# Shifted and seam copies of normalised image planes: by SBUF-to-SBUF DMAs instead of by VectorE

## The chip, the cores and the metric

One Trainium2 chip, one NeuronCore of it. The metric is the device time of one execution in microseconds, as the median of several executions. Engines by their names in the profile: PE (TensorE matmul) and PEld (its weight loads), DVE (VectorE), ACT (ScalarE), POOL (GpSimd) and SP (SyncE, which here only issues DMAs).

## The reference

The input x holds 32 images of 192 channels and 32 x 32 pixels. Each image goes through two residual blocks.

```python
x = x + _L0_conv_ref(_gn(x), w_qkv, w_out, b_out)        # channel attention
x = x + _L1_conv_ref(_gn(x), proj_w, proj_b, off_w, off_b, mask_w, mask_b, gamma, beta)
```

`_gn` is a group norm over 32 groups of channels. The first block forms a 192 x 192 attention matrix of channels per image. The second block is a deformable 3 x 3 convolution: an ordinary 3 x 3 convolution of the normalised image gives 27 numbers a pixel (two offsets and a mask for each of nine taps); each tap then reads the image at its shifted position with bilinear weights; the result is multiplied by `proj_w`, normalised over the whole batch (all images) and put through a GELU.

## The kernel before, in words

**Pipeline.** Images are handled in pairs of phases. `part0(u, b, par)` prepares image b: statistics, the attention block, the second group norm, the offset convolution and the bilinear weights. `part1(b, par, more)` does the deformable convolution of image b in 48 units (u = 0 to 47). In each unit, part1 of image b also calls `part0(u, b + 1, 1 - par)`, so the preparation of the next image is spread by hand over the units of this one. Image 0 is prepared alone, ahead of all. `par` is the parity of the image; buffers with a `par` index are doubled. Every engine runs its own copy of this order (lines 336 to 349), and semaphores tie the copies together. A hardware loop covers two images a turn.

**A unit of part1.** GpSimd multiplies row and column weights into `sT` (line 1323; one for two units, a ring of three). PE transposes it into `sps` (`turn_s`, line 650, done for unit u + 2), ACT rounds that to fp16 as `sh` (line 887), DVE subtracts to get the remainder `sl` (line 1142). PE then multiplies (lines 667 to 669). `sps` has two banks, so the transpose of unit u + 2 waits until `sl` of unit u is made (line 647). Beside this PE makes products of the planes with the projection weights, the z groups (lines 636 to 640), ten groups ahead; ACT and DVE split them likewise into `zh` (line 853) and `zl` (line 1136). From u = 38 on the z groups belong to the next image.

**The planes.** The second group norm of part0 gives the image as fp16 pieces in three planes of 128 partitions: `x2[0]` (first 128 channels, rounded), `x2[1]` (their remainder) and `x2[2]` (the other 64 channels, rounded in the lower half of the partitions, remainder in the upper). ACT writes the rounded pieces at units 30 to 33 and DVE the remainders, `residue`, at units 32 and 34 (line 999). Two more forms are needed. `x2s` has each plane moved by one pixel to the right and to the left within each image row, zero at the edge, for the left and right taps of the offset convolution. `x2w` has the last three and the first three rows of a plane side by side, for the z groups that lie across the image's seam. `move(k, b, par)` (line 1001) makes them with four DVE copies for plane k: lines 1005 and 1006 (31 of 32 columns of every row), 1008 and 1009 (seams). It is called at units 33, 35 and 36, ahead of nothing but the next unit's `sl` and `zl` in DVE's order:

```python
if u == 35:
    dve.wait_ge(xn_lo, 4 * b + 4)
    move(1, b, par)
if u == 36:
    move(2, b, par).then_inc(x2_moved, 1)
```

**Readers.** PE waits for `x2_moved` twice: before z group 0 of the next image, which reads `x2w` and which PE reaches in unit 38 of part1 (line 623), and before the offset convolution (line 572), 216 small matmuls (line 578) in units 38 and 39. From that follow, on the other engines, offsets, clipping, bilinear weights of the next image (lines 1096 to 1118 on DVE, 1307 on GpSimd).

**SP's queue** holds, for each image, in this order: `attended(b)`, the two stores of x1 and the three loads of the next image's x (at unit 26); and `convolved(b - 1)`, the two stores of y (line 431), which waits for unit 6 of the next part1.

**GpSimd** runs sT for the pairs of units p = 0 to 23, three ahead of PE at most; after the sT of pair p it does what `part0` has for units 2p - 4 and 2p - 3. At the start it zeroes the planes (line 1282).

Of the kernel before, what the change touches and what calls it, by code (L numbers as in the profile page):

```python
# [30 lines left out]
F32, F16, I32 = mybir.dt.float32, mybir.dt.float16, mybir.dt.int32  # L31
# [4 lines left out]
P = 128  # L36
C, H, W = 192, 32, 32
N = H * W
# [10 lines left out]
PAD_T, PAD_ROWS = 1, H + 2  # L49
WRAP = 3  # L50
# [32 lines left out]
def build(nc, x, w_qkT, w_v, w_outT, b_out, w_off, b_off, w_proj, proj_b, gamma, beta,  # L83
          avg, cy, cx, eye, out):
    NB = x.shape[0]
# [4 lines left out]
    with ExitStack() as ctx:  # L90
        def sb(name, shape, dt=F32):
            return ctx.enter_context(nc.sbuf_tensor(name, shape, dt))
# [4 lines left out]
        def sem(name):  # L97
            return ctx.enter_context(nc.semaphore(name))
# [48 lines left out]
        rsum = sb("rsum", [P, 2])  # L147
        rinv = sb("rinv", [P, 2])

        x2s = [sb(f"x2s_{n}", [P, 2, PAD_ROWS * W], F16) for n in ("hi_a", "lo_a", "hilo_b")]  # L150

        x2w = [sb(f"x2w_{n}", [P, 2, 2 * WRAP * W], F16) for n in ("hi_a", "lo_a", "hilo_b")]

        x2 = [sb(f"x2_{n}", [P, 2, PAD_ROWS * W], F16) for n in ("hi_a", "lo_a", "hilo_b")]
        off = sb("off", [P, 2, TILES, J])
        ay = sb("ay", [P, 2, TILES * TAPS, R])
        bx = sb("bx", [P, 2, TILES * TAPS, W])
# [66 lines left out]
        mx_ps = sem("mx_ps")  # L224
        x1_sb = sem("x1_sb")
        x1_stored = sem("x1_stored")
        x2_moved = sem("x2_moved")
        off_ps = sem("off_ps")
        off_sb = sem("off_sb")
# [58 lines left out]
        def inner(t, par):  # L288

            return t[:, par, PAD_T * W:PAD_T * W + N]  # L290
# [87 lines left out]
        def first(b):  # L378
            return isinstance(b, int) and b == 0
# [28 lines left out]
        @block.sync  # L408
        def _(sp):
            def load_x(b):  # L410
                for dst, src in ((xin[:, 0], x[b, 0:P]), (xin[0:CB, 1], x[b, P:C]), (xin[CB:P, 1], x[b, P:C])):
                    sp.dma_start(dst, src).then_inc(x_loaded, 16)

            load_blocks(sp, off_stage, w_off, weights_in)
            load_blocks(sp, proj_stage, w_proj, weights_in)
            sp.dma_start(eye32[:, :], eye).then_inc(const_in, 16)
            load_x(0)
            sp.dma_start(avg_sb[:, :, :], avg.rearrange("p (a b) -> p a b", a=4)).then_inc(const_in, 16)
            sp.dma_start(cy_sb[:, :], cy).then_inc(const_in, 16)
            sp.dma_start(cx_sb[:, :, :], cx.rearrange("p (k x) -> p k x", k=TAPS)).then_inc(const_in, 16)  # L420

            def attended(b, more=True):
                sp.wait_ge(x1_sb, 4 * b + 4)
                sp.dma_start(x1_dram[b, 0:P], x1[:, 0]).then_inc(x1_stored, 16)
                sp.dma_start(x1_dram[b, P:C], x1[0:CB, 1]).then_inc(x1_stored, 16)
                if more:
                    load_x(b + 1)

            def convolved(b):
                sp.wait_ge(y_final, b + 1)  # L430
                sp.dma_start(y_dram[b, 0:P], ych[:, 0]).then_inc(y_stored, 16)
                sp.dma_start(y_dram[b, P:C], ych[0:CB, 1]).then_inc(y_stored, 16)

            attended(0)
            with sp.Fori(1, NB - 2, 2) as b:
                attended(b)
                convolved(b - 1)
                attended(b + 1)
                convolved(b)
            attended(NB - 1, False)  # L440
            convolved(NB - 2)


            def load(dst, src, q, slot, i):
                if i < 2:
                    sp.dma_start(dst[slot][i], src[2 * q + i, 0:P]).then_inc(f_loaded[slot], 16)
                else:
                    for h in range(2):
                        sp.dma_start(dst[slot][i][CB * h:CB * h + CB], src[2 * q + h, P:C])\
                          .then_inc(f_loaded[slot], 16)  # L450

            def load_pair(q, slot):
                for i in range(3):
                    load(fin_y, y_dram, q, slot, i)
                    load(fin_x, x1_dram, q, slot, i)

            sp.wait_ge(y_stored, 32 * (NB - 2))
            sp.wait_ge(x1_stored, 32 * NB)
            sp.wait_ge(xn_hi, 4 * NB)
            for i in range(3):  # L460
                load(fin_y, y_dram, 0, 0, i)
            load(fin_x, x1_dram, 0, 0, 0)
            convolved(NB - 1)
            sp.wait_ge(bn_var, 1)
            for i in range(1, 3):
                load(fin_x, x1_dram, 0, 0, i)
            for slot in range(1, FIN):
                load_pair(slot, slot)
            sp.wait_ge(y_stored, 32 * NB)

            def load_next(r_, slot):
                sp.wait_ge(f_stored[slot], 64 * r_)
                load_pair(FIN * r_ + slot, slot)

            with sp.Fori(1, ROUNDS) as r_:
                for slot in range(FIN):
                    load_next(r_, slot)
            for slot in range(PAIRS - ROUND_ENDS):
                load_next(ROUNDS, slot)
# [455 lines left out]
        def _(dve):  # L935
# [62 lines left out]
                dve.wait_ge(xn_hi, 4 * b + 2 * n + i + 1)  # L998
                dve.tensor_tensor(lo, xn[:, 0] if i == 0 else xn[CB:P, 1], hi, ALU.subtract).then_inc(xn_lo, 1)

            def move(k, b, par):

                rows = lambda v: v.rearrange("p (h w) -> p h w", w=W)
                src = rows(inner(x2[k], par))
                dve.tensor_copy(rows(inner(x2s[k], 0))[:, :, 1:W], src[:, :, 0:W - 1])
                dve.tensor_copy(rows(inner(x2s[k], 1))[:, :, 0:W - 1], src[:, :, 1:W])
                seam = rows(x2w[k][:, par])
                dve.tensor_copy(seam[:, 0:WRAP], src[:, H - WRAP:H])
                return dve.tensor_copy(seam[:, WRAP:2 * WRAP], src[:, 0:WRAP])  # L1009

            def zero_outside(hat, rows, tiles):

                for t in tiles:
# [8 lines left out]
            def part0(u, b, par):  # L1022
# [54 lines left out]
                    group_variance(1, b)  # L1077
                if u == 32:
                    residue(0, inner(x2[1], par), inner(x2[0], par), 1, b)
                if u == 33:  # L1080
                    if not first(b):
                        dve.wait_ge(off_ps, b)
                    move(0, b, par)
                if u == 34:
                    residue(1, inner(x2[2], par)[CB:P], inner(x2[2], par)[CB:P], 1, b)
                if u == 35:
                    dve.wait_ge(xn_lo, 4 * b + 4)
                    move(1, b, par)
                if u == 36:
                    move(2, b, par).then_inc(x2_moved, 1)  # L1090
                if u == 40:
                    dve.wait_ge(off_ps, b + 1)
                    if not isinstance(b, int) or b >= 2:
# [184 lines left out]
        def _(pool):  # L1278
            pool.memset(mhalf[:, :], -0.5)
            pool.memset(minus[:, :], -1.0)  # L1280
            for t in (*x2, *x2s):
                ins = pool.memset(t[:, :, :], 0.0)
            ins.then_inc(pool_setup, 1)
            pool.wait_ge(pool_setup, 1)
            pool.wait_ge(const_in, CONST_DMAS * 16)
# [9 lines left out]
            def part0(u, b, par):  # L1295
                if u == 5:
                    group_rstd(0, b)
                if u == 29:
                    group_rstd(1, b)
                if u == 41:  # L1300
                    column_distance(0, b, par)

            def column_distance(q, b, par):
                if q == 0:
# [85 lines left out]
```

## Time and profile before

| What | Value |
|---|---|
| Median of 3 runs (lowest to highest) | 4268.0 us (4258.34 to 4275.98) |
| The profiled execution, first to last instruction | 4284.4 us |
| PE busy | 3630.2 us (85%) |
| DVE busy | 2649.3 us (62%) |
| ACT busy | 2110.5 us (49%) |
| POOL busy | 1410.9 us (33%) |
| Mean granted TensorE clock | 0.939 of full speed |
| DMA | 172.85 MB, mean 40 GB/s |

The profile shows one execution, 4284.4 us of span with no more than the launch around it, 16 us longer than the median run. Busy time is the share of the span in which an engine ran an instruction; PE's matmuls overlap, so its share says little of how near it is to its peak. A wait is idle time of an engine together with the instruction that released it; "issue" stands for time in which nothing that the profile shows held the engine.

### The profile page before, as it was taken

The numbers are of one execution on the slowest core, as the hardware profiler recorded it, in microseconds if no ns is written. First come the engines' busy times: TensorE is split into PE (matmuls) and PEld (weight loads), VectorE is DVE, ScalarE is ACT, GpSimd is POOL, SyncE is SP. The second block draws the span as 40 slices with busy tenths as digits, with TensorE's granted clock in tenths as the row PEclk, the third lists the DMA queues.
The fourth block names the chain that finished last, engine by engine and source line by source line (L and its number), as shares of the span: only waits on it lengthen the run. The fifth ranks groups of instructions, "written<-read, shape, count | busy, mean of one in ns | idle before, by whom it ended". The sixth has DMA issues, their size and how long they took to land.

```text
span 4284.4 us, 109949 instructions
## 1 busy us (share of the span) xinstructions
PE 3630.2 (85%) x38338; PEld 3094.4 (72%) x38338; DVE 2649.3 (62%) x5834; ACT 2110.5 (49%) x4790; POOL 1410.9 (33%) x1165
## 2 busy tenths in 40 slices
PE   3999898999989899998989989898998989899700
PEld 2787777877777778777777877777787777778700
DVE  3666666666666666666666666666666666666522
ACT  1555554555455455545545554554555455445432
POOL 1333332333333233333333333333333333333311
PEclk8999999999999999999999999999999999999955
DMA  2000000000000000000000000000000000000298
GB/s 59 18 27 10 28 27 20 27 27 27 10 27 27 20 27 26 27 10 27 27 20 27 26 27 16 21 27 20 27 26 27 21 16 27 27 20 16 60 361 301
DMA packets 50975, 172.85 MB, mean 40 GB/s; under 512 B 9664, under 2 KB 10880, under 8 KB 50176
## 3 DMA queue, kind: packets, MB, share of 16 engines
q1 hardware_dynamic: 39584, 136.75, 10.6%
q0 software_dynamic: 7168, 25.17, 1.5%
q8 instruction: 426, 6.98, 0.7%
q14 instruction: 373, 3.06, 0.2%
q10 hardware_dynamic: 3424, 0.90, 0.1%
HBM read 87.29 MB, written 75.50 MB: 38 GB/s over the span
## 4 chain that ended last, share of the span: by engine, by line
PE 63%; DVE 13%; issue 13%; ACT 4%; DMA 4%; DVEq 1%; ACTq 1%; SPq 1%; POOL 0%; POOLq 0%
PE sps L650 10%; PE acc L667 6%; PE acc L668 6%; PE acc L669 6%; PE l L578 4%; PE zps L636 3%; DVE zl L1136 3%; PE zps L640 3%; PE zps L637 3%; PE zps L638 3%; PE zps L639 3%; DMA xn<-x_scratch 2%; DVE sl L1142 2%; DVE ych L1204 2%; PE l L510 1%
## 5 line engine op out<-in xcount | busy, mean ns | idle before, releaser
L1323 POOL TENSOR_TENSOR sT<-ay,bx 128x768 f32<-128x768 f32 x768 | 1148.1, 1505 | 1615.3 <-PE sps L650 1547.9
L1142 DVE TENSOR_TENSOR sl<-sps,sh 128x384 f16<-128x384 f32 x1536 | 847.1, 552 | 743.7 <-ACT sh L887 740.3
L887 ACT CAST sh<-sps 128x384 f16<-128x384 f32 x1536 | 741.7, 483 | 915.4 <-PE sps L650 905.9
L667 PE MATMUL acc<-zh,sh 128*128 128x192 f16 x4608 | 1155.7, 251 | 0.3 <-ACT ypm L910 0.3
L668 PE MATMUL acc<-zl,sh 128*128 128x192 f16 x4608 | 1155.5, 251 | 0.0
L669 PE MATMUL acc<-zh,sl 128*128 128x192 f16 x4608 | 1155.2, 251 | 0.0
L650 PE MATMUL sps<-eye,sT 128*128 128x128 f32 x4608 | 808.0, 285 | 322.0 <-issue 218.2
L853 ACT CAST zh<-zps 128x288 f16<-128x288 f32 x1536 | 620.1, 404 | 699.6 <-PE zps L640 672.6
L1136 DVE TENSOR_TENSOR zl<-zps,zh 128x288 f16<-128x288 f32 x1536 | 693.9, 452 | 423.0 <-ACT zh L853 415.7
L650 PEld LDWEIGHTS sps<-eye,sT 128*128 128x128 f32 x4608 | 544.5, 143 | 451.9 <-issue 229.4
L667 PEld LDWEIGHTS acc<-zh,sh 128*128 128x128 f16 x4608 | 459.0, 100 | 37.5 <-issue 35.9
L668 PEld LDWEIGHTS acc<-zl,sh 128*128 128x128 f16 x4608 | 459.1, 100 | 20.9
L669 PEld LDWEIGHTS acc<-zh,sl 128*128 128x128 f16 x4608 | 459.1, 100 | 1.6
L636 PE MATMUL zps<-wpr_h,x_hi_a 128*128 128x288 f16 x1344 | 392.1, 292 | 0.8 <-DVE zl L1136 0.3
L637 PE MATMUL zps<-wpr_l,x_hi_a 128*128 128x288 f16 x1344 | 390.8, 291 | 0.0
L638 PE MATMUL zps<-wpr_h,x_lo_a 128*128 128x288 f16 x1344 | 390.1, 290 | 0.0
L639 PE MATMUL zps<-wpr_h,x_hilo_b 128*128 128x288 f16 x1344 | 389.7, 290 | 0.0
L640 PE MATMUL zps<-wpr_l,x_hilo_b 128*128 128x288 f16 x1344 | 389.7, 290 | 0.0
L1307 POOL TENSOR_TENSOR bx<-off,cx_sb 128x576 f32<-128x576 f32 x128 | 155.3, 1213 | 459.4 <-DVE off L1103 459.4
L1289 POOL TENSOR_TENSOR rstd<-gvar,mhalf 128x2 f32<-128x2 f32 x64 | 44.8, 700 | 582.0 <-DVE gvar L993 582.0
L578 PE MATMUL l<-wof,x2s_hi_a 128*128 128x54 f16 x1536 | 183.0, 186 | 9.8 <-DVE x2w_hilo_b L1009 9.8
L578 PE MATMUL l<-wof,x2s_lo_a 128*128 128x54 f16 x1536 | 182.8, 186 | 0.0
(200 smaller groups left out, 6498.0 us busy)
## 6 DMA issues: line engine op xcount, KB each, us to landing
xin<-in_x SPq DMA_DIRECT2D x32, 512.0 KB, 5.5
xin<-in_x SPq DMA_DIRECT2D x64, 256.0 KB, 5.9
x_scratch<-x SPq DMA_DIRECT2D x32, 512.0 KB, 2.8
y_scratch<-ych SPq DMA_DIRECT2D x32, 512.0 KB, 2.7
zh<-y_scratch SPq DMA_DIRECT2D x20, 512.0 KB, 11.0
zl<-x_scratch SPq DMA_DIRECT2D x20, 512.0 KB, 12.0
out<-zh POOLq DMA_DIRECT2D x20, 512.0 KB, 8.8
x_scratch<-x SPq DMA_DIRECT2D x32, 256.0 KB, 3.5
```

Of the source, the lines that this page charges most:

```text
L578: mm = pe.matmul(o, src[:, row * W:(row + ROWS_T) * W], wof[:, m, k].rearrange("p i j -> p (i j)"), start=(k == 0 and n == 0), stop=(k == ...
L636: pe.matmul(o, at(0), wpr_h[:, 0, ky, n], start=True, stop=False)
L637: pe.matmul(o, at(0), wpr_l[:, 0, ky, n], start=False, stop=False)
L650: mm = pe.transpose(sps[u % 2][:, kx * P:(kx + 1) * P], sT[:, g, kx, c * P:(c + 1) * P], eye32[:, :])
L667: pe.matmul(acc[:, 0:C], s_h, zh[:, j, ky, z], start=start and kx == 0, stop=False)
L668: pe.matmul(acc[:, 0:C], s_h, zl[:, j, ky, z], start=False, stop=False)
L669: mm = pe.matmul(acc[:, 0:C], s_l, zh[:, j, ky, z], start=False, stop=stop and kx == 2)
L853: act.copy(z_piece(zh, g, par), zps[:, g % 2, 0:KO // 2]).then_inc(z_hi, 1)
L887: act.copy(sh[:, u % S_RING].rearrange("p k n -> p (k n)"), sps[u % 2][:, 0:3 * P]).then_inc(s_hi, 1)
L1136: dve.tensor_tensor(z_piece(zl, g, par), zps[:, g % 2, 0:KO // 2], z_piece(zh, g, par), ALU.subtract)\
L1142: dve.tensor_tensor(one(sl), sps[u % 2][:, 0:3 * P], one(sh), ALU.subtract).then_inc(s_lo, 1)
L1323: pool.tensor_tensor(sT[:, p % ST_RING].rearrange("p k (r x) -> p k r x", r=R), a, x_, ALU.mult)\
```

## The change

The tensors of the three planes are joined into one tensor for each form, so that one access pattern takes all three planes. DVE's `move` is gone. SP, behind the x1 stores and the loads, waits for the last residue (`xn_lo`) and issues four DMAs: two for the seams, and two that copy the whole plane as one run of 1023 elements a partition and plane, one element to the right and one to the left. A run like that carries the last pixel of a row into the first column of the next one (or the reverse), so GpSimd, once all four have landed, sets that one column to zero in both moved forms with two memsets, and then raises `x2_moved`. PE's waits are as before.

```diff
-        x2s = [sb(f"x2s_{n}", [P, 2, PAD_ROWS * W], F16) for n in ("hi_a", "lo_a", "hilo_b")]
-
-        x2w = [sb(f"x2w_{n}", [P, 2, 2 * WRAP * W], F16) for n in ("hi_a", "lo_a", "hilo_b")]
-
-        x2 = [sb(f"x2_{n}", [P, 2, PAD_ROWS * W], F16) for n in ("hi_a", "lo_a", "hilo_b")]
+        x2s_all = sb("x2s", [P, 3, 2, PAD_ROWS * W], F16)
+        x2w_all = sb("x2w", [P, 3, 2, 2 * WRAP * W], F16)
+        x2_all = sb("x2", [P, 3, 2, PAD_ROWS * W], F16)
+        x2s, x2w, x2 = [[t[:, k] for k in range(3)] for t in (x2s_all, x2w_all, x2_all)]
...
+            def shift(b, par):
+
+                sp.wait_ge(xn_lo, 4 * b + 4)
+                plane = x2_all[:, :, par, PAD_T * W:PAD_T * W + N]
+                flat_plane = lambda h: x2s_all[:, :, h, PAD_T * W:PAD_T * W + N]
+                sp.dma_start(x2w_all[:, :, par, 0:WRAP * W], plane[:, :, N - WRAP * W:N]).then_inc(x2_shifted, 16)
+                sp.dma_start(x2w_all[:, :, par, WRAP * W:2 * WRAP * W], plane[:, :, 0:WRAP * W])\
+                  .then_inc(x2_shifted, 16)
+                sp.dma_start(flat_plane(0)[:, :, 1:N], plane[:, :, 0:N - 1]).then_inc(x2_shifted, 16)
+                sp.dma_start(flat_plane(1)[:, :, 0:N - 1], plane[:, :, 1:N]).then_inc(x2_shifted, 16)
+
...
             attended(0)
+            shift(0, 0)
             with sp.Fori(1, NB - 2, 2) as b:
                 attended(b)
+                shift(b, 1)
                 convolved(b - 1)
                 attended(b + 1)
+                shift(b + 1, 0)
                 convolved(b)
             attended(NB - 1, False)
+            shift(NB - 1, (NB - 1) % 2)
             convolved(NB - 2)
...
-            def move(k, b, par):
-
-                rows = lambda v: v.rearrange("p (h w) -> p h w", w=W)
-                src = rows(inner(x2[k], par))
-                dve.tensor_copy(rows(inner(x2s[k], 0))[:, :, 1:W], src[:, :, 0:W - 1])
-                dve.tensor_copy(rows(inner(x2s[k], 1))[:, :, 0:W - 1], src[:, :, 1:W])
-                seam = rows(x2w[k][:, par])
-                dve.tensor_copy(seam[:, 0:WRAP], src[:, H - WRAP:H])
-                return dve.tensor_copy(seam[:, WRAP:2 * WRAP], src[:, 0:WRAP])
...
-                if u == 33:
-                    if not first(b):
-                        dve.wait_ge(off_ps, b)
-                    move(0, b, par)
                 if u == 34:
                     residue(1, inner(x2[2], par)[CB:P], inner(x2[2], par)[CB:P], 1, b)
-                if u == 35:
-                    dve.wait_ge(xn_lo, 4 * b + 4)
-                    move(1, b, par)
-                if u == 36:
-                    move(2, b, par).then_inc(x2_moved, 1)
...
-            for t in (*x2, *x2s):
-                ins = pool.memset(t[:, :, :], 0.0)
+            for t in (x2_all, x2s_all):
+                ins = pool.memset(t[:, :, :, :].rearrange("p k h n -> p (k h n)"), 0.0)
...
+                if u == 37:
+                    edges(b)
                 if u == 41:
                     column_distance(0, b, par)
+
+            def edges(b):
+
+                pool.wait_ge(x2_shifted, 64 * b + 64)
+                pool.sem_inc(edges_due, 1)
+                for h in range(2):
+                    rows = x2s_all[:, :, h, PAD_T * W:PAD_T * W + N].rearrange("p k (r w) -> p k r w", w=W)
+                    ins = pool.memset(rows[:, :, :, (W - 1) * h:(W - 1) * h + 1], 0.0)
+                ins.then_inc(x2_moved, 1)
```

## Rows read from the trace of the kernel before

**Rows 1.** The page's head and its first part: busy time of each engine.

```profile
span 4284.4 us, 109949 instructions
PE 3630.2 (85%) x38338; PEld 3094.4 (72%) x38338; DVE 2649.3 (62%) x5834; ACT 2110.5 (49%) x4790; POOL 1410.9 (33%) x1165
```

**Rows 2.** Waits of PE: engine line waited for: us in total, times, longest.

```profile
PE sps L650 <- issue: 218.2, 46, 8.8
PE sps L650 <- DVE sl L1142: 96.1, 125, 1.2
```

**Rows 3.** DVE lines 999, 1005, 1008, 1009: duration ns min/median/max, first and last start.

```profile
L999 DVE TENSOR_TENSOR x_hilo_b<-xn,x_hilo_b x32: 1221/1222/1224, 94.0 to 3938.2; 64x1024 f16<-64x1024 f32 x32
...
L1005 DVE COPY x2s_hi_a<-x_hi_a x32: 408/410/419, 92.9 to 3935.2; 128x992 f16<-128x992 f16 x32
...
L1008 DVE COPY x2w_hi_a<-x_hi_a x32: 173/1446/1450, 93.6 to 3935.8; 128x96 f16<-128x96 f16 x32
...
L1008 DVE COPY x2w_hilo_b<-x_hilo_b x32: 163/167/173, 96.8 to 3944.0; 128x96 f16<-128x96 f16 x32
...
L1009 DVE COPY x2w_hilo_b<-x_hilo_b x32: 172/174/182, 96.9 to 3944.1; 128x96 f16<-128x96 f16 x32
```

**Rows 4.** Timeline of DVE, last image prepared: start us, us, instruction [idle before].

```profile
3935.16 0.41 DVE L1005 COPY x2s_hi_a<-x_hi_a 128x992 f16<-128x992 f16 x1
...
3937.30 0.54 DVE L1142 TENSOR_TENSOR sl<-sps,sh 128x384 f16<-128x384 f32 x1
```

**Rows 5.** Timeline of ACT in the same stretch.

```profile
3934.92 0.52 ACT L887 CAST sh<-sps 128x384 f16<-128x384 f32 x1
```

**Rows 6.** Timeline of PE in the same stretch; line 650 opens a unit.

```profile
3931.27 0.49 PE L650 MATMUL sps<-eye,sT 128*128 128x128 f32 x3
...
3932.95 0.49 PE L650 MATMUL sps<-eye,sT 128*128 128x128 f32 x3
...
3934.93 0.55 PE L650 MATMUL sps<-eye,sT 128*128 128x128 f32 x3
...
3937.90 0.55 PE L650 MATMUL sps<-eye,sT 128*128 128x128 f32 x3 [1.07 <-DVE sl L1142]
...
3943.08 0.55 PE L650 MATMUL sps<-eye,sT 128*128 128x128 f32 x3 [1.07 <-DVE sl L1142]
...
3944.40 0.29 PE L636 MATMUL zps<-wpr_h,x_hi_a 128*128 128x288 f16 x1
```

**Rows 7.** Timeline of SP: the two stores of y of one image.

```profile
3868.62 0.34 SPq L431 DMA_DIRECT2D y_scratch<-ych  x1
3869.17 0.54 SPq L432 DMA_DIRECT2D y_scratch<-ych  x1
```

**Rows 8.** DMA queues (packets, MB, share of 16 engines) and issues (KB, median us to landing).

```profile
q10 hardware_dynamic: 3424, 0.90, 0.1%
...
y_scratch<-ych SPq DMA_DIRECT2D x32, 256.0 KB, 3.3
```

**Rows 9.** Stretches of stores, then of loads: us, busy by engine, PEclk, DMA share, GB/s.

```profile
3799.00:3800.00 1.00, 1.00 (x13) 0.82 (x10) 0.83 (x4) 0.74 (x2) 0.00 (x0) 1.00 1.06 381
...
3801.00:3802.00 1.00, 1.00 (x9) 0.96 (x9) 0.59 (x2) 0.35 (x2) 0.00 (x0) 1.00 0.73 188
```

**Rows 10.** Timeline of PE at the end of an image.

```profile
239.91 0.90 PE L650 MATMUL sps<-eye,sT 128*128 128x128 f32 x3 [4.36 <-issue]
```

**Rows 11.** The stretch behind that gap; columns as in rows 9.

```profile
240.00:244.00 4.00, 4.00 (x21) 3.37 (x22) 0.64 (x2) 0.88 (x2) 0.00 (x0) 0.50 0.00 0
```

**Rows 12.** Timeline of POOL: a zeroing at the start; sT and column distance near 3940.

```profile
8.34 1.91 POOL L1282 MEMSET x2s_lo_a<- 128x2176 f16 x1
...
3940.74 1.69 POOL L1323 TENSOR_TENSOR sT<-ay,bx 128x768 f32<-128x768 f32 x1 [3.50 <-PE sps L650]
3956.70 1.16 POOL L1307 TENSOR_TENSOR bx<-off,cx_sb 128x576 f32<-128x576 f32 x1 [14.28 <-DVE off L1103]
```

More of the change, by code:

```diff
@@ L226, in build @@
         x1_stored = sem("x1_stored")
+        x2_shifted = sem("x2_shifted")
+        edges_due = sem("edges_due")
         x2_moved = sem("x2_moved")
```

## The prediction

> **What bounds the kernel now.** I read the page's head first, then PE's own waits, then the twelve copies by line, and at last the timelines of DVE, ACT and PE through one stretch. PE is busy 85% of a span of 4284.4 us [rows 1], so a gain or a loss has to reach PE. In PE's waits [rows 2] two things stand out: 218.2 us in 46 waits that nothing in the profile ends, which sit at the ends of images, and 96.1 us in 125 short waits for the subtraction `sl` on DVE. The second kind is where this change acts. The copies by line [rows 3] show that the shifted planes are cheap (410 ns for 992 columns), while the seam copy of 96 columns takes 1446 ns in the median on the first plane (the second's is alike) and 167 ns on the third, which runs when GpSimd is idle. Apart from image 0 the durations hardly differ over 32 images, so one image can stand for all.
>
> In the timeline of the last image [rows 4] DVE begins the first block of copies at 3935.16 and takes up `sl` again at 3937.30; ACT had delivered its input (`sh`, line 887) at 3934.92 + 0.52 = 3935.44 [rows 5]. On PE [rows 6] a unit takes 1.68 us where nothing holds it (3931.27 to 3932.95), but unit 36 begins at 3937.90, after a 1.07 us wait for `sl`, and unit 38 at 3943.08, behind the second block. Group 0 of the next image's z product, the first reader of all copies, starts at 3944.40, the third block having ended at 3944.1 + 0.17 [rows 3]. So the copies cost PE time by holding up `sl`, not by being late themselves.
>
> **What goes.** Without the first block, `sl` of unit 36 starts at about 3935.5 instead of 3937.30. The second residue (line 999 on `x_hilo_b`) started 0.9 us after that `sl` (3938.2 - 3937.30, [rows 3, 4]), so now at 3936.4, and ends 1.22 us later, at 3937.6 instead of 3939.4. PE then runs its units at its own pace: unit 35 at 3934.93 as before (the first residue, which stays, holds that one), 36 at 3936.66, 37 at 3938.4, 38 at 3940.1, and it is ready for z group 0 about 1.1 us later, at 3941.2. If the copies were there by then, PE would have gained 3944.4 - 3941.2 = **3.2 us** an image. DVE's own 6 us of copies has no other value: past this point its next work waits for PE.
>
> **What comes.** The new chain is: last residue, SP wakes, four DMAs, GpSimd wakes, two memsets, PE. It starts at 3937.6. Break-even with today's 3944.4 is a chain of **6.8 us**; to be hidden altogether it must take 3.6 us.
>
> No row shows a copy from SBUF to SBUF, so I bound it. Bytes: 2 x 128 x 3 x 1023 x 2 and 2 x 128 x 3 x 96 x 2, together 1.72 MB, in 1536 rows of 2046 and 192 bytes. Fixed part: the two stores of y, 0.79 MB, are issued 0.55 us apart [rows 7] and the second lands 3.3 us after its issue [rows 8], so 3.85 us in all; at the 381 GB/s of a store stretch [rows 9] the bytes are 2.06 us of that and the rest 1.8 us is issue, start and landing. Rate: 381 GB/s where only stores run, 188 GB/s in a stretch where loads run [rows 9]. That gives 4.5 or 9.1 us for the bytes. The copies read SBUF as the stores do, write SBUF as the loads do, and their rows are half as long, so I take the middle, 285 GB/s or 6.0 us. The 768 seam rows go to 16 engines, 48 each; by queue q10, 3424 packets of 263 bytes in some 0.1% of the engines' span [rows 8, 1], a packet takes 10 to 30 ns, so 0.5 to 1.4 us, about what that rate gives for their bytes. GpSimd: a memset of 2176 columns takes 1.91 us [rows 12], so one of 96 columns some 0.1 to 0.2; two with the wake-ups at both ends 0.4 us; SP's wake-up 0.1. Sum 0.1 + 1.8 + 6.0 + 0.4 = **8.3 us**, with ends of 5.7 (a rate above the stores', and issues that overlap) and 11.4.
>
> So PE starts z group 0 at 3937.6 + 8.3 = 3945.9 instead of 3944.4: **1.5 us late** per image, though it arrived 3.2 us early. It now stands still from about 3941.4 to 3945.9, 4.5 us in one piece.
>
> **The clock.** The rows show what such a gap does: after the idle 4.36 us before a unit at an image's end [rows 10] PE's granted clock is 0.50 in the following 4 us [rows 11], which is the 1.2 GHz level of 1.2 and 2.4. The 46 waits of that kind make 218.2 us, 4.7 us each on average [rows 2], so it is about the length of my new gap. In this kernel the work behind the new gap is 216 matmuls of the offset convolution, and PE alone sets their pace. Half rate for the 4 us of that window loses 2 us; a spell twice as long would lose 4. The window shown need not hold the whole spell, so I take **2.7 us**, with bounds of 0 and 4.
>
> Per image 1.5 + 2.7 = 4.2 us, times 31 images that overlap the one before: 130 us. Image 0 has no cover: its last residue ends at 94.0 + 1.2 = 95.2 and its copies at 96.9 + 0.17 = 97.1 [rows 3], now at 103.5, so +6. **Sum +136 us.** The profiled span is 4284.4 us, 16.4 above the median of the runs shown, 4268.0; I carry the difference over unscaled: 4404.
>
> **Edits without a price.** The zeroing at the start clears as many columns in two instructions as before in six, under the wait for weights. The joined tensors change addresses alone. DVE's dropped wait on `off_ps` is implied by its wait at unit 40 of the image before. On SP the four DMAs stand behind the x1 stores and the next load, which SP issues at unit 26, eight units before the last residue, and ahead of the store of y, which waits for unit 6 of the next image. On GpSimd the new wait holds back sT of rows 21 and 22 of 24; PE wants the first of them two units and the whole offset convolution later, and GpSimd has 14.28 us idle before the column distances [rows 12]. If that cover were gone, each sT would cost its 1.69 us.
>
> **Rivals.** (a) *The copies are quick, the chain takes 5.7 to 7.0 us.* Then PE is released at 3943.3 to 3944.6 and the gap on PE is 2 to 3.4 us, shorter than the one whose clock the rows show to fall. It decides at 6.8 us. For it: the stores' 381 GB/s, with no transfer beside these. At 5.7 us: -1.1 x 31 + 3 = -31, 4237; at 6.8 about 4275. Against it: four issues in line on one queue, short rows, an odd start in the row.
> The Trainium skill's page "DMA: Bandwidth & Descriptors" (sections "Anatomy of one DMA" and "Why small descriptors are slow (HBM only)") fits a transfer, on GpSimd's path, by about 2 us plus its bytes at 436 GB/s, and holds that copies between SBUF and SBUF don't pay for short descriptors. By that page the bytes take 3.9 us, the chain, as an estimate, 6.4 us and the kernel some 4260; no run here shows its rate.
> (b) *The copies are slow*, at the loads' 188 GB/s: 11.4 us, 4.6 us late, clock loss 3.2 (a longer gap), so 7.8 x 31 + 8 = +250, 4518. For it: writes into SBUF are the loads' side; against: a load also reads HBM.
> (c) *The clock holds.* Lateness alone: 1.5 x 31 + 6 = +53, 4321. For it: the new gap is only just as long as those that lost the clock. This is also what comes if the copies were not in PE's way after all and PE reaches group 0 no earlier than now: the gap is then 1.5 us.
>
> **How the numbers follow.** Forecast (7 to 10.5 us, with the clock) 0.52, its own range 4360 to 4490; (a) 0.21, of which half lies below 4247; (b) 0.14; (c) 0.13. About 0.5% (21 us) is what a measurement can tell here. Faster: the quick half of (a), 0.10. Same: the rest of (a), 0.11. Slower: forecast, (b) and (c), 0.79. The range leaves out the quick half of (a) and most of (b): 4260 to 4480.
>
> **What would show it.** Right: the `sl` waits of PE (96.1 us) shrink to under half; a new wait of 4 to 5 us a time, 31 times, before group 0 of z on the seam tile or on the offset convolution, put down to GpSimd's memset; clock 0.50 behind it; units 36 to 38 at 1.7 us; the last shifted plane landing 5 to 7 us after its issue. The forecast is wrong if that wait is under 3 us, or if the matmuls behind it run at full clock, or if SP takes over 1 us for each issue, which would make it worse.

## The result and the profile after

| | Before | After |
|---|---|---|
| Median of 4 runs (lowest to highest) | 4271.99 us (4258.34 to 4276.58) | 4400.65 us (4390.76 to 4413.5) |
| Ratio (95% interval) | 1 | 1.0306 (1.0287 to 1.0326) |
| Profiled span | 4284.4 us | 4397.7 us |
| Mean granted TensorE clock | 0.939 | 0.916 |

The kernel became 3.1% slower, by 129 us between the medians and by 113.3 us between the profiled spans. First the head and first part of the page of after, which answer to [rows 1]:

```profile
span 4397.7 us, 109785 instructions
PE 3667.5 (83%) x38338; PEld 3152.5 (72%) x38338; DVE 2497.5 (57%) x5450; ACT 2107.3 (48%) x4790; POOL 1417.3 (32%) x1225
```

VectorE (DVE) was relieved of 152 us, and it did the kernel no good. PE has as many instructions as before and is busy 37.3 us longer, though it computes nothing more. The waits of PE, which answer to [rows 2] (engine, line, what was waited for: us in total, times, longest):

```profile
PE sps L666 <- issue: 208.6, 46, 9.2
PE zps L652 <- POOL x2s L1308: 156.5, 31, 6.7
...
PE sps L666 <- DVE sl L1139: 19.9, 32, 0.9
...
PE l L594 <- POOL x2s L1308: 16.3, 1, 16.3
```

The waits for `sl` went from 96.1 to 19.9 us, as the change wants. In their place stands one wait an image, 156.5 us in 31 times, 5.0 us each, before z group 0. Line 1308 is GpSimd's memset, the last link of the new chain. One image shows it whole; it is the last one prepared, as in [rows 4 to 6]. On PE (line 666 opens a unit, lines 652 to 656 are a z group):

```profile
4041.26 0.49 PE L666 MATMUL sps<-eye,sT 128*128 128x128 f32 x3
...
4043.24 0.55 PE L666 MATMUL sps<-eye,sT 128*128 128x128 f32 x3
...
4044.98 0.49 PE L666 MATMUL sps<-eye,sT 128*128 128x128 f32 x3
...
4046.66 0.49 PE L666 MATMUL sps<-eye,sT 128*128 128x128 f32 x3
...
4048.34 0.49 PE L666 MATMUL sps<-eye,sT 128*128 128x128 f32 x3
...
4054.26 0.42 PE L652 MATMUL zps<-wpr_h,x 128*128 128x288 f16 x1 [4.69 <-POOL x2s L1308]
...
4060.50 0.53 PE L666 MATMUL sps<-eye,sT 128*128 128x128 f32 x3
```

Units 36 to 38 (4044.98, 4046.66, 4048.34) follow unit 35 at a pace of 1.7 us. Before, unit 36 opened 2.97 us behind unit 35, and unit 38 another 5.18 us behind that (3934.93, 3937.90 and 3943.08, [rows 6]). From the opening of unit 35 (4043.24) PE needs 6.33 us until it has nothing left (4054.26 - 4.69 = 4049.57). Before, group 0 began 9.47 us behind unit 35 (3944.40 - 3934.93, [rows 6]); now it begins 11.02 us behind it. What it waits for begins with the last residue, on DVE's timeline:

```profile
4044.73 1.22 DVE L1015 TENSOR_TENSOR x<-xn,x 64x1024 f16<-64x1024 f32 x1
```

Then come SP's four issues, on its own timeline:

```profile
4045.98 0.66 SPq L435 DMA_DIRECT2D x2w<-x  x1
4046.68 0.68 SPq L436 DMA_DIRECT2D x2w<-x  x1
4047.40 0.64 SPq L438 DMA_DIRECT2D x2s<-x  x1
4048.08 0.63 SPq L439 DMA_DIRECT2D x2s<-x  x1
```

And the two memsets, on POOL's:

```profile
4053.19 0.93 POOL L1308 MEMSET x2s<- 128x96 f16 x2 [11.56 <-DMA x2s<-x]
```

And the DMA view of the stretch from 4045 to 4055, in 40 slices of 0.25 us:

```profile
DMA  0000000007609519999999999999992000000000
GB/s 0 0 0 0 0 0 33 0 0 160 135 0 189 106 65 393 409 417 434 409 401 401 393 401 417 401 426 417 409 401 90 0 0 0 0 0 0 0 0 0
```

Read together these give the chain, from the end of the last residue (4045.95) to group 0 (4054.26), 8.31 us. SP wakes after 0.03. The first bytes of the copies move in the tenth slice, 1.3 us after the first issue (the 33 GB/s in the seventh slice are one packet of instructions). The seams' packets trickle until 4048.5, for SP takes 0.7 us from one issue to the next, and the planes' packets begin at 4048.7, again 1.3 us behind their issue. Four microseconds at 393 to 434 GB/s bring the planes over by 4052.7. GpSimd begins 0.5 us later, its two memsets take 0.93 us, and PE starts 0.14 us behind them.

What the standstill costs beyond itself is in the granted clock. The stretches around it, with the columns of [rows 9], PE's granted clock third from the right:

```profile
4051.00:4052.00 1.00, 0.00 (x0) 0.00 (x0) 0.00 (x0) 0.00 (x0) 0.00 (x0) 1.00 1.07 415
4052.00:4053.00 1.00, 0.00 (x0) 0.00 (x0) 0.00 (x0) 0.00 (x0) 0.00 (x0) 0.91 0.59 225
4053.00:4054.00 1.00, 0.00 (x0) 0.00 (x0) 0.00 (x0) 0.00 (x0) 0.81 (x3) 0.50 0.00 0
4054.00:4058.00 4.00, 3.74 (x47) 3.29 (x48) 1.06 (x2) 0.40 (x1) 2.75 (x3) 0.50 0.01 4
4058.00:4062.00 4.00, 4.00 (x91) 3.91 (x89) 0.33 (x1) 0.48 (x1) 0.00 (x0) 0.79 0.02 4
```

PE works at the 1.2 GHz level (0.50) from its restart until about 4059.7 (0.79 over 4 us leaves 1.7 us at half). The same 128x288 matmul takes 0.42 instead of 0.29 us, and from group 0 to the opening of unit 39 PE needs 6.24 us (4060.50 - 4054.26). One more row of the kernel before has that opening at 3948.19, 3.79 us behind group 0:

```profile
3948.19 0.53 PE L650 MATMUL sps<-eye,sT 128*128 128x128 f32 x3
```

**The balance.** Read off PE's timeline for all 31 images that overlap another, in means: group 0 starts 16.73 us after the opening of unit 32, before 14.82, so **1.91 us late**. From there to unit 39 it takes 6.14 us, before 3.78, so **2.36 us for the clock**. That makes 4.27 us, but from image to image the period grew by 3.49 us only (127.10 against 123.61): **0.78 us are given back** around the change of image, most of it 0.22 in unit 47 and 0.46 in unit 1. Unit 1 runs behind the long wait at the image's end, and its length follows the clock: over the 31 images of either trace it is 1.69 us plus 0.49 of the time that PE is at half rate in it, and that time is 2.01 us in the mean before and 1.06 after. Of the kernel before, as timed beside run 4, the execution with the highest granted clock (0.942) took 4252.8 us and the one with the lowest (0.939) 4281.0, so a part of this can belong to the profiled execution alone. Image 0, which nothing covers, reaches group 0 5.0 us later (109.72 against 104.70); PE's wait before its offset convolution, 16.3 us in the list above, was 9.8. 3.49 x 31 + 5.0 = 113.2 us, the difference of the spans.

### The profile page after: what moved, and what is told of

It reads as the page before. It is cut to its first block, busy times and chain, and to the rows that moved or that the text cites. A ratio compares the mean times of both kernels' runs of the same rounds, so it can differ in the third digit from the quotient of the medians.

```text
span 4397.7 us, 109785 instructions
## 1 busy us (share of the span) xinstructions
PE 3667.5 (83%) x38338; PEld 3152.5 (72%) x38338; DVE 2497.5 (57%) x5450; ACT 2107.3 (48%) x4790; POOL 1417.3 (32%) x1225
## 4 chain that ended last, share of the span: by engine, by line
PE 65%; issue 9%; DVE 8%; DMA 8%; ACT 5%; SPq 2%; DVEq 1%; POOL 1%; ACTq 1%; POOLq 0%
PE sps L666 10%; PE acc L683 6%; PE acc L684 6%; PE acc L685 6%; PE l L594 5%; DMA x2s<-x 4%; PE zps L652 3%; PE zps L656 3%; PE zps L653 3%; PE zps L655 3%; PE zps L654 3%; DMA xn<-x_scratch 2%; DVE zl L1133 2%; PE l L526 1%; PE l L525 1%
## 5 line engine op out<-in xcount | busy, mean ns | idle before, releaser
L1331 POOL TENSOR_TENSOR sT<-ay,bx 128x768 f32<-128x768 f32 x768 | 1136.7, 1492 | 1435.9 <-PE sps L666 1368.7
L652 PE MATMUL zps<-wpr_h,x 128*128 128x288 f16 x1344 | 391.8, 291 | 83.2 <-POOL x2s L1308 82.8
L653 PE MATMUL zps<-wpr_l,x 128*128 128x288 f16 x1344 | 392.1, 292 | 0.0
L654 PE MATMUL zps<-wpr_h,x 128*128 128x288 f16 x1344 | 392.0, 292 | 0.0
L655 PE MATMUL zps<-wpr_h,x 128*128 128x288 f16 x1344 | 391.9, 292 | 0.0
L656 PE MATMUL zps<-wpr_l,x 128*128 128x288 f16 x1344 | 391.9, 292 | 0.0
L594 PE MATMUL l<-wof,x2s 128*128 128x54 f16 x4608 | 229.9, 198 | 16.3 <-POOL x2s L1308 16.3
L594 PEld LDWEIGHTS l<-wof,x2s 128*128 128x128 f16 x4608 | 213.3, 105 | 19.9 <-POOL x2s L1308 16.4
## 6 DMA issues: line engine op xcount, KB each, us to landing
zh<-y_scratch SPq DMA_DIRECT2D x20, 512.0 KB, 10.1
```

The source lines that it names most:

```text
L594: mm = pe.matmul(o, src[:, row * W:(row + ROWS_T) * W], wof[:, m, k].rearrange("p i j -> p (i j)"), start=(k == 0 and n == 0), stop=(k == ...
L653: pe.matmul(o, at(0), wpr_l[:, 0, ky, n], start=False, stop=False)
L654: pe.matmul(o, at(1), wpr_h[:, 0, ky, n], start=False, stop=False)
L1331: pool.tensor_tensor(sT[:, p % ST_RING].rearrange("p k (r x) -> p k r x", r=R), a, x_, ALU.mult)\
```

## The experiments

The theory after the result: the copies on DVE did cost PE some 3 us an image; the new chain is too long by 1.9 us, and the standstill that it makes costs another 2.3 us in clock. Each run below was timed beside the kernel before on the same chip, and its ratio is to the median of that.

**1. The ceiling: no copies at all.** The four DMAs and SP's wait are gone.

```diff
             def shift(b, par):
-                sp.wait_ge(xn_lo, 4 * b + 4)
...
+                pass
...
-                pool.wait_ge(x2_shifted, 64 * b + 64)
+                pool.wait_ge(xn_lo, 4 * b + 4)
```

> The four DMAs are left out (the moved forms and the seams keep zeros, so the offsets and the seam products are not the reference's); GpSimd waits for the last residue alone and zeroes the columns as before. Theory (the copies held up the subtraction on VectorE, 3.05 us an image in units 36 to 38): no wait is left before z group 0, units 36 to 38 take 1.7 us, 31 x 3.05 = 95 us under the kernel before, so about 4175 us. Rival (the copies lay beside PE's work, and the change lost time by its wait alone): the kernel before's time, about 4270.

Measured: 4163.52 us, 0.9725 (0.9703 to 0.9748). No wait before z group 0 is left among PE's; group 0 starts 11.5 us after unit 32 instead of 14.8. So VectorE's copies were worth 115 us, 20 more than expected; units 35 to 38 alone are 3.30 us an image shorter, 102 us in all, and the prediction's gain of 3.2 us an image is real: the change loses through what it puts in their place, not for want of a gain.

**2. Keep PE busy in the wait.** If the clock is lost to the standstill, matmuls that nobody reads, ahead of the wait, should bring it back. First with fp16 fillers:

```diff
-                if g == 0:
-                    pe.wait_ge(x2_moved, b + 1)
...
+                if g == 0:
+                    if not first(b):
+                        for _ in range(46):
+                            pe.matmul(zps[:, 0, KO // 2:512], wpr_h[:, 0, 0, 0:P], wpr_h[:, 0, 0, 0:512 - KO // 2],
+                                      start=True, stop=True)
+                    pe.wait_ge(x2_moved, b + 1)
```

> The changed kernel; PE runs 46 matmuls of 224 columns on constant weights into unused columns, some 4.4 us, where it stands still before z group 0. Theory (the gap of 4.7 us costs the clock, and the clock costs 2.3 us an image behind it): granted clock 1.00 behind the wait, the 216 matmuls of the offset convolution at 25 ns each again, 31 x 2.3 = 71 us less, some of it given back at the image's end: 4325 to 4360. Rival (the slow convolution comes of the new copies, by reads of fresh data or by addresses): the clock rises and the time stays at 4400 or above.

Measured: 4416.72 us, 1.0315 (1.0286 to 1.0343): the expectation failed. The waits of PE say why only in part:

```profile
PE sps L670 <- issue: 187.7, 31, 9.1
PE zps L656 <- POOL x2s L1312: 65.4, 31, 2.6
```

The fillers end 2.1 us before the chain does, in the mean, because the chain itself grew, from 8.67 to 10.1 us. And in 24 of 31 images the clock fell even behind these short gaps. In the image released at 1381.16, after 2.01 us of idling, the granted clock was:

```profile
1379.00:1381.00 2.00, 0.15 (x2) 0.00 (x0) 0.00 (x0) 0.00 (x0) 0.83 (x3) 1.00 0.02 8
1381.00:1383.00 2.00, 1.84 (x20) 1.68 (x21) 0.59 (x2) 0.40 (x1) 2.00 (x3) 0.73 0.00 0
1383.00:1385.00 2.00, 2.00 (x50) 2.00 (x47) 0.47 (x1) 0.00 (x0) 0.73 (x1) 0.50 0.00 0
```

Here the clock fell after PE had started again, and stayed down for 3.4 us. Then with fewer, longer fillers, fp32 and 192 columns wide, in the same place:

```diff
+                        for _ in range(15):
+                            pe.matmul(zps[:, 0, KO // 2:KO // 2 + C], eye32[:, :],
+                                      avg_sb[:, :, :].rearrange("p a b -> p (a b)")[:, 0:C], start=True, stop=True)
```

> As the run with the filled wait, with 15 fp32 matmuls of 192 columns in place of the 46 short ones, so that PE's program grows by 30 instructions instead of 92 and the fetch of its next instructions stays where it was. Theory (the gap costs the clock): the chain stays at 8.7 us, what is left of the wait is under 0.7 us, the granted clock stays 1.00 behind it and the offset convolution takes 7.3 us as in the kernel before instead of 8.7; 31 x 2.2 = 68 us less than the change, 4335 (4315 to 4355). Rival (the slow convolution has another cause): 4400.

Measured: 4313.67 us, 1.0104 (1.0083 to 1.0124), 2.0 points of ratio below the change although its chain is longer (9.30 us in the mean, where 8.7 was expected; the time lies 1 us under the expected range). Its waits of PE:

```profile
PE sps L670 <- issue: 186.5, 31, 8.7
PE zps L656 <- POOL x2s L1312: 26.3, 16, 1.8
```

Three stretches around a gap of 1.71 us that ended at 3849.19:

```profile
3844.00:3848.00 4.00, 3.48 (x22) 3.18 (x20) 0.00 (x0) 0.00 (x0) 0.00 (x0) 1.00 0.48 180
3848.00:3852.00 4.00, 2.81 (x79) 2.71 (x80) 1.06 (x2) 0.40 (x1) 3.56 (x4) 1.00 0.00 0
3852.00:3856.00 4.00, 4.00 (x114) 3.87 (x111) 1.24 (x3) 0.88 (x2) 0.00 (x0) 1.00 0.02 4
```

The clock stays at 1.00 in every one of the 31 images, and from group 0 to unit 39 PE takes 3.78 us again, to the hundredth what it took before. So the 2.36 us of the balance are the clock's, and they are caused by the standstill. The period is 124.25 us, 2.85 less than the change's: 2.36 for the clock, less 0.63 because group 0 starts later, and 1.1 given back at the change of image, where 15 of 46 waits of PE have gone. The last part was not foreseen; the half-rate time around the change of image falls with it, from 8.4 to 6.3 us an image, and why the waits are gone stays open.

**What made the chain longer.** PE waits in only 16 of the 31 images in this kernel. Two neighbouring images, the DMA view of the stretch of their copies: in the first PE waited, in the second not.

```profile
q8 instruction: 1, 0.02, 0.9%
issues: line engine op xcount, KB each, median us to landing
x2s<-x SPq DMA_DIRECT2D x2, 767.2 KB, 6.3
```

The second, one image later:

```profile
q14 instruction: 1, 0.01, 0.3%
issues: line engine op xcount, KB each, median us to landing
x2s<-x SPq DMA_DIRECT2D x2, 767.2 KB, 4.4
```

The kernel's own instructions are loaded by the same 16 DMA engines (the last column is a share of them). Where a 16 KB packet of queue q8 runs while the packets of the planes do (16 images here), their last packet ends 15.7 us or more after the opening of unit 32, and 15.2 us or less where none does. In the profile of the change it is 5 images of 31, and these are the five with the longest chains (9.5 to 10.3 us against 8.2 to 8.6); with 46 fillers it is 29 of 31, the fillers being more instructions to load. No image of these three traces breaks the pattern, nor does one of run 4's below (8 images of 31, their last packet at 15.9 us or later, against 15.2 or less). No run moved such a packet and nothing else, so the cause is argued from the coincidence in 124 images and not shown by an experiment.

**3. The order of the DMAs.** The planes are issued ahead of the seams.

```diff
+                sp.dma_start(flat_plane(0)[:, :, 1:N], plane[:, :, 0:N - 1]).then_inc(x2_shifted, 16)
+                sp.dma_start(flat_plane(1)[:, :, 0:N - 1], plane[:, :, 1:N]).then_inc(x2_shifted, 16)
                 sp.dma_start(x2w_all[:, :, par, 0:WRAP * W], plane[:, :, N - WRAP * W:N]).then_inc(x2_shifted, 16)
...
-                sp.dma_start(flat_plane(0)[:, :, 1:N], plane[:, :, 0:N - 1]).then_inc(x2_shifted, 16)
-                sp.dma_start(flat_plane(1)[:, :, 0:N - 1], plane[:, :, 1:N]).then_inc(x2_shifted, 16)
```

> The changed kernel with the two plane DMAs issued ahead of the two seam DMAs. Theory (SP's issues stand in line at 0.7 us each, and the planes' bytes begin only behind the seams' issues): the bytes begin 1.4 us earlier, the chain falls from 8.7 to about 7.4 us: 31 x 1.3 = 40 us less, 4360, with the clock still lost behind a gap of 3.5 us; if the clock holds then, 4290. Rival (the chain is set by the bytes and the landing): 4400.

Measured: 4391.17 us, 1.0272 (1.0248 to 1.0296). The wait of PE:

```profile
PE zps L652 <- POOL x2s L1308: 145.8, 31, 5.8
```

And the seams among the DMA issues (KB each, median us to landing):

```profile
x2w<-x SPq DMA_DIRECT2D x64, 72.0 KB, 4.9
```

The planes start 1.4 us earlier, but the seams' bytes now come behind them (landing 4.9 us after their issue, not 2.2), and GpSimd waits for all four, so the chain shrinks by 0.35 us alone. The rival was the nearer, and the ratio's interval still touches that of the change (1.0287 to 1.0326).

**4. The memsets.** They are left out, so the moved planes keep a neighbour's pixel in their edge column.

```diff
-                for h in range(2):
-                    rows = x2s_all[:, :, h, PAD_T * W:PAD_T * W + N].rearrange("p k (r w) -> p k r w", w=W)
-                    ins = pool.memset(rows[:, :, :, (W - 1) * h:(W - 1) * h + 1], 0.0)
-                ins.then_inc(x2_moved, 1)
+                pool.sem_inc(x2_moved, 1)
```

> The changed kernel without the two memsets of the edge columns (the edges keep the neighbouring row's pixel, so the offsets at the edges are not the reference's); GpSimd raises the semaphore at once. Theory (the memsets stand in the chain with the 0.9 us that the trace shows, not with the 0.3 I had put): z group 0 starts 0.8 us earlier, the gap stays near 4 us and the clock is still lost: 31 x 0.8 = 25 us under the change, 4375 (4365 to 4390); if the shorter gap keeps the clock, 4310. Rival (the memsets hide behind the landing): 4400.

Measured: 4367.17 us, 1.0227 (1.0187 to 1.0266). The chain falls to 7.90 us in the mean, the wait to this:

```profile
PE zps L652 <- POOLq L1306: 132.7, 31, 5.7
```

4.3 us of standstill still cost the clock. So the memsets are worth 0.8 of the 8.67 us; without them the kernel stays slower than before.

**5. Take the readers out of the way.** Z group 0 needs only the seams. It waits for those alone, and the offset convolution, which needs the moved planes, goes as a whole to unit 40, with GpSimd's memsets ahead of it there.

```diff
-                if 38 <= u < 40:
-                    for t in range(TILES // 2):
-                        offset_conv(TILES // 2 * (u - 38) + t, b, par)
+                if u == 40:
+                    for t in range(TILES):
+                        offset_conv(t, b, par)
...
-                    pe.wait_ge(x2_moved, b + 1)
+                    pe.wait_ge(x2_seamed, 32 * b + 32)
```

> The changed kernel with its readers moved apart: z group 0 waits for the two seam DMAs alone, the whole offset convolution stands in unit 40 instead of 38 and 39, and GpSimd waits for the planes behind the sT for units 44 and 45. Theory (nothing is wrong with the DMAs but their length of 8.7 us): the chain lies beside units 38 and 39, PE waits under 1.5 us, the clock holds, and the 3.05 us an image stay won less half a microsecond: 31 x 2.7 = 84 us under before, 4190 (4175 to 4215). Rival (the later convolution makes the next image's weights late): a new wait of PE for sT or for its subtraction at the image's end of 2 us, about 4250; and a seam that lands late adds up to 0.5 us an image.

Measured: 4212.77 us, 0.9844 (0.9826 to 0.9863): with the same four DMAs and memsets the kernel is now faster than before. The waits of PE:

```profile
PE sps L667 <- issue: 215.6, 46, 9.1
PE l L595 <- POOL x2s L1309: 55.1, 32, 16.4
```

Less image 0's 16.4 us, 1.25 us an image are left of the chain (38.7 / 31), and behind none of these waits does the clock fall: the whole profile has 36 half-rate spells, against 66 with the change and 35 before. Its control moves the offset convolution in the kernel before, with nothing else changed:

> The kernel before with the offset convolution whole in unit 40 instead of in halves in 38 and 39, nothing else. A control for the run of the change with the convolution later. Theory (that run gained by hiding the chain, not by the convolution's place): within 15 us of the kernel before. Rival (the place alone is worth something, as the subtractions of units 38 and 39 run without it): 4240.

Measured: 4230.73 us, 0.9898 (0.9878 to 0.9919). Here the expectation failed: the place alone is worth 38 us in the kernel before, mostly in two steps away from the copies. Unit 43 to 44 is 0.69 us shorter in the median. DVE's work on the offsets begins 1.41 us ahead of unit 42 instead of 0.67, its product `ay` (line 1107), which began well inside GpSimd's `bx` before, takes 0.45 us instead of 0.81, and PE no longer waits for `sl` there. The waits for `sl`, 96.1 us in 125 times in [rows 2], become:

```profile
PE sps L650 <- DVE sl L1142: 78.4, 95, 1.3
```

Unit 1 to 2 is 0.55 us shorter, and that is the clock again: PE is at half rate for 0.96 us of it in the mean instead of 2.01. Why that spell ends earlier is open. So of the 65 us that run 5 gained, some 38 would have come without the DMAs, if the two gains add.

**6. Which of the twelve copies cost.** Two rows of the kernel before stand behind the next two runs. On POOL's timeline:

```profile
3935.55 1.69 POOL L1323 TENSOR_TENSOR sT<-ay,bx 128x768 f32<-128x768 f32 x1 [2.23 <-PE sps L650]
```

And on DVE's:

```profile
3935.84 1.45 DVE L1008 COPY x2w_hi_a<-x_hi_a 128x96 f16<-128x96 f16 x1
```

The seam copy begins inside GpSimd's sT and ends as sT ends (3937.29 and 3937.24). It does so again at 3941.02, beside the sT from 3940.74, while the third seam copy, with no sT beside it, takes 167 ns [rows 3]. The Trainium skill's page "SBUF — State Buffer", section "Who interferes with whom", says that VectorE in its two-port copy modes and GpSimd hold a shared pair of ports in turn, each for a whole instruction, and that ScalarE waits for nobody; for VectorE these rows agree, and the next two runs try it. First only the seams by DMA, the planes staying on DVE and without memsets (against the changed kernel):

```diff
-                sp.dma_start(flat_plane(0)[:, :, 1:N], plane[:, :, 0:N - 1]).then_inc(x2_shifted, 16)
-                sp.dma_start(flat_plane(1)[:, :, 0:N - 1], plane[:, :, 1:N]).then_inc(x2_shifted, 16)
...
+                dve.tensor_copy(rows(inner(x2s[k], 0))[:, :, 1:W], src[:, :, 0:W - 1])
+                return dve.tensor_copy(rows(inner(x2s[k], 1))[:, :, 0:W - 1], src[:, :, 1:W])
```

> VectorE copies the planes as in the kernel before (two copies a plane, 0.4 us each), SP copies the seams alone by the two small DMAs, no memset on GpSimd; z group 0 waits for the seams, the offset convolution for VectorE. Theory (on VectorE only the seam copies are dear, at 1.45 us beside GpSimd's sT, and on the DMA engines only the planes' bytes are): a block of copies falls from 2.1 to 0.8 us, which the units hide, the seams land 3 us after the last residue, and z group 0 waits under 0.5 us: 31 x 2.8 = 87 us under before, 4190 (4170 to 4210). Rival (the plane copies hold up the subtraction as well): about half of that, 4230.

Measured: 4183.7 us, 0.9798 (0.978 to 0.9817). Then the kernel before with the seam copies of the first two planes on ScalarE and no DMA:

```diff
+                if u in (35, 36):
...
+                    act.copy(seam[:, 0:WRAP], src[:, H - WRAP:H])
+                    act.copy(seam[:, WRAP:2 * WRAP], src[:, 0:WRAP]).then_inc(x2_seamed, 1)
...
+                if k < 2:
+                    return
```

> The kernel before with the seam copies of the first two planes on ScalarE in units 35 and 36, the rest on VectorE; no DMA. Theory (1.45 us a seam copy comes of VectorE waiting while GpSimd runs sT, and not of the copy's form): on ScalarE the same copies take 0.2 to 0.3 us beside sT, the waits of PE for the subtraction in units 36 and 38 go, and the time comes near the run with the seams by DMA: 4195 (4180 to 4220). Rival (any engine that reads or writes these tiles waits for GpSimd): ScalarE's copies take over 1 us and the time stays at about 4270.

Measured: 4191.88 us, 0.9815 (0.9791 to 0.9839). The copies on ScalarE (ns: min, median, max; first and last start):

```profile
L836 ACT COPY x2w_hi_a<-x_hi_a x32: 255/274/275, 94.2 to 3853.3; 128x96 f16<-128x96 f16 x32
```

By their times both expectations held. But the trace of the second run hardly tries its theory: of the four seam copies on ScalarE only the first of an image begins while an sT runs, and that 0.09 us before the sT's end. On POOL's timeline, then on ACT's:

```profile
3851.68 1.69 POOL L1335 TENSOR_TENSOR sT<-ay,bx 128x768 f32<-128x768 f32 x1 [2.23 <-PE sps L652]
...
3853.28 0.27 ACT L836 COPY x2w_hi_a<-x_hi_a 128x96 f16<-128x96 f16 x1
```

That ScalarE does not wait beside an sT is thus not shown here. That VectorE does is shown by a copy that neither run meant to change. With the slow seam copies gone, the first copy of the third plane comes earlier and now begins inside an sT, in this run as in the one before. On POOL's timeline, on DVE's, and that copy in all images (ns: min, median, max):

```profile
3855.73 1.69 POOL L1335 TENSOR_TENSOR sT<-ay,bx 128x768 f32<-128x768 f32 x1 [2.36 <-PE sps L652]
...
3856.84 0.87 DVE L1015 COPY x2s_hilo_b<-x_hilo_b 128x992 f16<-128x992 f16 x1
...
L1015 DVE COPY x2s_hilo_b<-x_hilo_b x32: 412/871/873, 96.3 to 3856.8; 128x992 f16<-128x992 f16 x32
```

It takes 0.87 us in the 31 images in which it begins inside an sT, and 0.41 in image 0, in which it does not. In the kernel before it began behind the sT and took 0.41 us in all 32. The two seam copies of before follow the same rule: 1.45 us in the 31 images in which they begin inside an sT, 0.17 in image 0. So the price goes with the moment at which VectorE's copy begins, and not with its form.

The two slow seam copies, 2.9 us of DVE's 6 us an image, carried about 80 of the 115 us of the ceiling; the plane copies, which all began outside an sT and took 0.41 to 0.44 us each, little. Where the seams go matters less than that they leave DVE at that moment; no run tried to keep them on DVE at another one.

**7. The best of both.** Seams by DMA, planes on DVE, offset convolution in unit 40.

> The run with the seams by DMA and the planes by VectorE, with the offset convolution whole in unit 40. Theory (two separate gains: VectorE's seam copies, 85 us, and the place of the convolution, 38 us in the control, of which the part behind the image's end of 0.6 us an image is won already): 31 x 0.8 = 24 us under the run without it, 4160 (4145 to 4170). Rival (both gains are the same one): 4184.

Measured: 4168.27 us, 0.9767 (0.9737 to 0.9798). Its interval overlaps that of the seams by DMA alone, and the profiled spans are alike (4170.6 and 4169.6 us), so these two are not told apart; either is 2 to 2.3% faster than before. The traces show why the gains did not add: unit 43 is 0.66 us shorter again, but unit 1 is at half rate for 2.08 us in the mean, against 0.90 with the seams by DMA alone, and is 0.57 us longer.

## Why the prediction was right

By its own steps, with the last image beside the means:

- **Bound and gain.** The step held. Unit 35 to the end of PE's ready work was to take 6.3 us and took 6.33; the last residue was to end 2.7 us behind unit 35 and ended 2.71 behind it. Run 1 shows the gain by itself (3.30 us an image in units 35 to 38, 3.2 forecast). That the cost sat in the seam copies rather than in the plane copies was in the rows (1446 against 410 ns), and run 6 shows it and why.
- **The chain.** The sum held (8.3 us forecast, 8.31 in the last image, 8.67 in the mean), the terms did not, and it was luck that their errors cancelled. Bytes: forecast 6.0 us at 285 GB/s, measured 4.0 us for the planes at 393 to 434 GB/s; the middle between loads and stores was the wrong choice, the stores were nearer. Fixed part: forecast 1.8, measured 2.7 from SP's first issue to the planes' first packet, because two issues of 0.7 us stand ahead of the planes', and 0.5 from the last packet to the memset. GpSimd: forecast 0.4, measured 0.93 for the two memsets, whose records overlap, and 0.14 to PE. A memset of 96 columns scattered over rows takes 0.66 us in the median, not the share of the 1.91 us that 2176 columns in one piece take [rows 12].
- **Rival (a), quick copies.** Right in its rate and wrong in its chain. The Trainium skill's page "DMA: Bandwidth & Descriptors", in the sections that the prediction names, gives 436 GB/s and holds short descriptors harmless between SBUF and SBUF; the slices of 393 to 434 GB/s with 2046-byte rows agree with the rate, and of the 192-byte rows no stretch shows one. The chain of 5.7 to 7.0 us that the rival put beside this rate was exceeded by what is not transfer: issues in line, and the memsets. Nor would its gap of 2 to 3.4 us have been safe for the clock, as the rival took it: in run 2 with fp16 fillers the clock fell behind 24 of the 27 gaps of 2.0 to 2.6 us.
- **Lateness.** 1.5 us forecast, 1.55 in the last image (11.02 - 9.47), 1.91 in the mean. The rest is the five images with an instruction packet among the copies, which no step had, and 0.2 us more in every second image.
- **The clock.** Right in kind and nearly in size: 2.7 us forecast, 2.36 measured. The granted clock of 0.50 behind the wait rules out (c), and run 2 with fp32 fillers shows that the standstill is the cause.
- **What no step had.** 0.78 us an image came back around the change of image, 0.46 of it by a shorter half-rate spell in unit 1, which the forecast could not know. The total, 3.49 x 31 + 5 = 113 us in the profiled runs, is below the 136 of the sum; that the medians differ by 129 us goes with a profiled run of before that lay 12 us above its median, and to that extent it is luck that the forecast of 4404 lies 3 us beside the median of 4400.65.
- **Edits without a price.** None showed: the waits of PE for sT and the stores did not grow.

## What to carry to other kernels

Before an engine is relieved of copies, ask which of them is slow and why: here two of twelve, each begun while GpSimd was inside an instruction, held about 80 of 115 us, and moving these alone, to DMA or to ScalarE, gave 2% where moving all twelve lost 3%. A DMA in place of a copy brings issue, start and landing onto the path, so price it as a chain from the last writer to the first reader and put work between, as run 5 did. A standstill of PE that grows to several microseconds is paid for a second time in the clock; in the three runs whose gaps before group 0 were 3.7 us and more (the change, 3 and 4), this was so in every image.

## What the runs showed that was not expected

- Loading the kernel's own instructions seems to delay its copies: wherever one 16 KB packet ran beside the planes' packets, they ended 1 to 2 us later, and with 46 more matmuls an image that was the rule rather than the exception.
- With fp16 fillers the clock fell behind 24 gaps of 2.0 to 2.6 us and held behind seven: three of 2.1 to 2.3 us and the four shorter ones (0.76 to 1.90). With fp32 fillers it held behind all 16 gaps, of which 15 were 1.7 to 1.8 us long and one 0.7. Whether the length of the gap or the kind of work before it decides isn't settled.
- Moving 216 matmuls by two units in the kernel before, away from the copies, gave 1.0%, about as much through the waits in unit 43 as through a shorter half-rate spell behind the change of image.
- How long that spell lasts in unit 1 differed between kernels, from 0.75 to 2.1 us of half rate in the mean, and was worth up to 0.7 us an image. It comes on top of what a change does elsewhere, and what sets it is open.
